# One VectorE operation of 512 columns per sigma in place of two of 256 in a delta-rule attention kernel

## The reference

```
def step(carry, seg):
    mem, z = carry
    qq, kk, vv = seg
    sigma_q = jax.nn.elu(qq) + 1.0
    scores = jnp.einsum('bhsk,bhtk->bhst', qq, kk) / scale
    att_dot = jax.nn.softmax(jnp.where(causal_mask, scores, -jnp.inf), axis=-1) @ vv
    att_mem = sigma_q @ mem / (sigma_q @ z)
    sigma_k = jax.nn.elu(kk) + 1.0
    delta = vv - sigma_k @ mem / (sigma_k @ z)
    mem_new = mem + jnp.einsum('bhsk,bhsv->bhkv', sigma_k, delta)
    z_new = z + sigma_k.sum(axis=-2, keepdims=True).transpose(0, 1, 3, 2)
    att = beta * att_mem + (1.0 - beta) * att_dot
    out = att.reshape(Bsz, SEG, H * DV) @ Wo
```

## Time and profile before

| | |
|---|---|
| median of 3 runs | 744.07 us (743.4 to 746.38) |
| profiled execution, its time | 749.53 us |
| profiled execution, its span | 747.7 us |
| TensorE busy, share of the span | 654.7 us, 88% |
| VectorE busy | 413.3 us, 55% |
| ScalarE busy | 339.4 us, 45% |
| GpSimd busy | 314.3 us, 42% |
| attention | from the start to about 441 us |
| its first stage | about 37 to 90 us |
| its last stage, without sigmas | about 390 to 441 us |

### The profile page before, as it was taken

One profiled execution on the slowest core, in us unless ns is written; L12 is line 12 of the kernel. 1 busy time (PEld: TensorE's weight loads), 2 busy tenths in 40 slices (PEclk: granted clock), 3 DMA queues, 4 the chain that ended last, 5 costly groups with the idle time before them and its releaser, 6 DMA issues. The chain is left out here.

```text
span 747.7 us, 12362 instructions
## 1 busy us (share of the span) xinstructions
PE 654.7 (88%) x4144; PEld 544.1 (73%) x4144; DVE 413.3 (55%) x1119; ACT 339.4 (45%) x834; POOL 314.3 (42%) x383
## 2 busy tenths in 40 slices
PE   4889989989989989989999986999999529984897
PEld 3668878979979879879789885875656318873554
DVE  6778495394593692781873727662222178355233
ACT  3666757566566665665665642123333203000210
POOL 4665644353344435425420305146665318110454
PEclk9999999999999999999999998899999859985799
DMA  8010110200100100100100414942233241028440
GB/s 265 20 57 29 30 56 1 64 29 20 46 29 29 35 28 28 35 28 30 35 1 4 110 64 161 411 145 85 93 85 85 98 153 45 1 77 317 131 113 22
DMA packets 31313, 57.89 MB, mean 77 GB/s; under 512 B 4670, under 2 KB 17952, under 8 KB 31264
## 3 DMA queue, kind: packets, MB, share of 16 engines
q1 hardware_dynamic: 24256, 42.03, 16.7%
q0 software_dynamic: 4896, 13.12, 6.1%
q10 hardware_dynamic: 2112, 2.10, 0.8%
HBM read 48.06 MB, written 10.09 MB: 78 GB/s over the span
## 5 line engine op out<-in xcount | busy, mean ns | idle before, releaser
L892 DVE RECIPROCAL denominators<-readings 128x2 f32<-128x2 f32 x128 | 21.2, 165 | 145.4 <-PE readings L567 144.7
L427 POOL TENSOR_TENSOR w_high<-xn,ones 128x256 fp32r<-128x256 f32 x84 | 53.2, 665 | 76.8 <-PE ahead L215 35.5
L567 PEld LDWEIGHTS readings<-memory_copy,sigma 128*128 128x128 f32 x512 | 75.1, 191 | 13.9 <-ACT memory_copy L764 5.0
L567 PE MATMUL readings<-memory_copy,sigma 128*128 128x129 f32 x512 | 78.9, 276 | 4.0 <-ACT memory_copy L764 3.8
L773 ACT ACTIVATE memory_reading<-readings,denominators 64x128 f32<-64x128 f32 x256 | 78.7, 357 | 5.3 <-DVE denominators L892 3.3
L764 ACT ACTIVATE memory_copy<-memory 128x258 f32<-128x258 f32 x128 | 50.2, 392 | 62.0 <-PE memory L577 48.0
L898 DVE SCALAR_TENSOR_TENSOR minus_delta<-readings,denominators,v 64x128 f32<-64x128 f32 x240 | 73.8, 347 | 4.2
L577 PE MATMUL memory<-minus_delta,sigma_k_tokens 128*128 128x129 f32 x480 | 73.2, 275 | 0.0
L1196 POOL DMA_INDIRECT xs_e<-rows_e,gather_at_e x46 | 44.9, 976 | 65.3 <-DVE scatter_at_e L1597 39.7
L1341 PE MATMUL up_e<-weights_e,xT_e 128*128 x184 | 68.8, 498 | 0.8 <-issue 0.8
L749 ACT ACTIVATE x<-ahead 128x512 f32<-128x512 f32 x60 | 35.9, 598 | 72.9 <-PE ahead L215 28.1
(11 more groups left out here) (267 smaller groups left out, 1438.5 us busy)
## 6 DMA issues: line engine op xcount, KB each, us to landing
weights_e<-experts SPq DMA_DIRECT2D x24, 608.0 KB, 11.8
xn<-L_attn_Wq SPq DMA_DIRECT2D x8, 512.0 KB, 3.8
xn<-L_attn_Wk SPq DMA_DIRECT2D x7, 512.0 KB, 3.8
xn<-L_attn_Wv SPq DMA_DIRECT2D x7, 512.0 KB, 3.9
wo<-L_attn_Wo SPq DMA_DIRECT2D x1, 2048.0 KB, 13.9
rows_e<-xn ACTq DMA_DIRECT2D x4, 512.0 KB, 7.9
x<-L_attn_x SPq DMA_DIRECT2D x4, 256.0 KB, 3.5
x<-L_attn_x SPq DMA_DIRECT2D x2, 512.0 KB, 3.6
```

The costliest lines, as they stand in the source:

```text
L427: last = pool.tensor_tensor(w_high[i][:, :, of], w_stage[:, :, of], one, ALU.mult)
L567: last = pe.matmul(KQ[g][:, hh * MC:(hh + 1) * MC], sqk[:, GROUP * g + hh, pair, 2 * par:2 * par + 2, :], mz[g][:, hh, :], start=True, sto ...
```

## The change

A query's sigma goes into `sigma` in one operation: the destination is blocks 1 and 2 of four tiles, 4 rows of 128 columns. A key's copy is one operation too: its destination is blocks 0 and 3 of four tiles, rows of 64 columns at two distances. The elements, their values and every wait and semaphore are the same; `sigma_ready` is raised by the one operation in place of the second of two.

```
-                def by_segment(t, par):
-                    return t.rearrange("p (a b c) -> p a b c", b=2, c=SEG)[:, :, par, :]
+                def by_segment(t):
+
+                    return t.rearrange("p (t a c) -> p t a c", a=2, c=SEG)
...
-                    for par in range(2):
-                        block_at = 1 + par if i == 0 else 3 * par
-                        out = sqk[:, h, half * TPH:(half + 1) * TPH, block_at, :]
-                        if i:
-                            last = dve.tensor_copy(out, by_segment(sk[h % 2][:, :], par))
-                        else:
-                            last = dve.scalar_tensor_tensor(out=out, in0=by_segment(natural, par), scalar=0.0,
-                                                            in1=by_segment(e[u % 2][:, :], par), op0=ALU.max, op1=ALU.add)
+                    tiles = slice(half * TPH, (half + 1) * TPH)
+                    if i:
+                        last = dve.tensor_copy(sqk[:, h, tiles, 0:4:3, :], by_segment(sk[h % 2][:, :]))
+                    else:
+                        last = dve.scalar_tensor_tensor(out=sqk[:, h, tiles, 1:3, :], in0=by_segment(natural), scalar=0.0,
+                                                        in1=by_segment(e[u % 2][:, :]), op0=ALU.max, op1=ALU.add)
                     last.then_inc(sigma_ready, 1)
```

## The result

| | before | changed |
|---|---|---|
| median | 744.78 us (743.4 to 746.38, 4 runs) | 737.62 us (734.67 to 738.12, 4 runs) |
| ratio, 95% interval | | 0.9891 [0.986, 0.9922] |
| profiled execution's span | 747.7 us | 736.1 us |
| first scores (L588) start at | 37.80 us | 39.80 us |
| first stage, to the next stage's first scores | 48.62 us | 49.43 us |

The medians differ by 7.2 us; by the ratio the change makes the kernel 8.1 us faster (5.8 to 10.4). The stage lengths are read from the timeline: first L588 of a stage to first L588 of the next.

What follows compares the result with a forecast made beforehand. TensorE bounds the kernel, so only its waits on VectorE's queue count. 1.10 us in each of six middle stages (6.6) plus 1.6 in the first stage gives 8.2 off 744.07: 735.9 us, range 732.0 to 740.5.

Steps and rivals of the forecast that it cites:

- What bounds it: Middle stage: TensorE's 2.72 us idle time is three waits of 1.68, 0.40 and 0.64 us, two directly behind sigmas.
- Undisturbed costs: Without GpSimd at work, a merged sigma takes 0.69 us against 0.76 for a pair, a merged copy 0.41 against 0.49.
- estimate of 157 ns: Saving per merged operation by the skill's fixed cost, 2.9 us more in six stages than the rows give; not adopted.
- Disturbed sigmas: Sigmas 2 and 3 beside GpSimd: one wait per operation, 1.10 us each merged, saving 0.38 and 0.60.
- The deduction of 0.18: Taken off each middle stage: L868 comes about 0.5 us earlier and may wait up to 0.42 for a w_low.
- the 1.28 of the sum: Middle stage's saving before deduction: 1.12 us from sigmas 0 to 3, 0.08 each from the copies of sigmas 4 and 5.
- The first stage: Saves 1.6 us: 1.4 from shorter disturbed sigmas 0 and 1, 0.2 of the later 1.39 wait, GpSimd being late next.
- the second rival: Waits for GpSimd only move: middle stages gain nothing, only the first stage keeps some, 743 us; chance 0.08.
- The start: Eight sigmas before the first stage: zero, since TensorE waits for GpSimd's value weights, which each sigma delays as before.
- the room of 3.8 us: Middle stage: GpSimd's probabilities end at 215.63, 3.8 us before TensorE is ready to turn them at 219.42.
- the lost pace: Rival: merged copies take 0.69 us, 0.20 more than the pair, making the kernel 739.7 us; chance 0.08.
- the half pace: Rival: merged sigmas with rows of 128 columns take up to 0.69 us more, making the kernel 754 us; chance 0.03.

## Why the prediction was right, point by point

- **What bounds it**: right. The three waits of a middle stage were where the gain came from: TensorE's idle time there fell from 2.72 to 1.53 us.
- **Undisturbed costs**: 0.69 and 0.43 measured, 0.69 and 0.41 forecast. So a merged operation saves 0.07 and 0.06 us. The trace decides against the estimate of 157 ns that the prediction drew from the Trainium skill, "VectorE: DVE Perf Modes", § The TRN2 errata. That estimate left out what the same page of the Trainium skill adds, § The DRAIN you can't avoid: an operation that is not held starts earlier.
- **Disturbed sigmas**: forecast 1.10 each, measured 0.99 and 1.11. One wait per operation was the right mechanism; the first of them stands beside GpSimd's `w_high` (L427), not `w_low`, and was 0.11 better.
- **The deduction of 0.18** for a lost moment of L868 did not occur: it took 0.41 at its new place as well, by the same luck of the moment as before. In the first stage, where I had not looked, the L869 of sigma 2 lost it and took 1.28 in place of 0.41. So a middle stage gained 1.38, not 1.10, which is the 1.28 of the sum and 0.1 from sigma 2. Six stages: 8.3, forecast 6.6.
- **The first stage** was wrong. Forecast 1.6 gained, 0.8 lost. The step that failed is "I count 1.4" for the two waits on ScalarE: they did vanish, but TensorE then waited 0.67 for GpSimd's `w_low`, and its wait in slot 8 grew from 1.39 to 2.72. TensorE's idle time in the stage is 5.6 us before and after: the waits only moved, as the second rival had it. I had named GpSimd as late next and sized it at nearly nothing. With the full clock the gain is 0.6; the fall of the clock took 1.2 to 1.4 us more.
- **The start** was wrong. Forecast 0 between -0.5 and +0.5, measured 2.0 lost: 1.5 by the clock, and 0.5 by a later value projection (27.60 to 28.10 us), which is no more than what moves there with no edit. The wait ahead of it grew from 1.65 to 2.21 us. The step that failed is that each sigma delays GpSimd "by as much as before": its eight splits there took 6.6 to 6.9 us in the four profiles with pairs at the start, 7.2 to 7.5 in the seven with everything merged, and 5.9 with the queries in quarters. The Trainium skill, "SBUF — State Buffer", § Who interferes with whom, has the loser blocked for the whole of the other's instruction. The rows show the longer holds: a `w_low` beside 512 columns took 1.18 us, and the wait, 2.21 in the changed kernel, was 1.56 with pairs at the start. I had taken from it that the sum of the delays stays the same, and these rows do not bear that out; in the middle stages the room of 3.8 us made it harmless.
- **The clock** had no term at all, and no reason was given for that.
- **The other rivals**: the merged sigma runs at 0.69 and the merged copy at 0.43, so neither the lost pace nor the half pace came true.
- **The whole**: 8.2 forecast, 7.2 measured by the medians and 8.1 by the ratio. By the trace attention gave 5.5. That the total is nearer is luck: by the two profiles it comes from what lies behind attention, which no step of mine accounts for.

## What to carry to other kernels

Before merging operations, look at what the engine beside them does at that moment, here GpSimd: the fixed cost saved here was 0.07 us, the waiting saved up to 0.6. The worth of a shorter operation is that of what stands behind it in its queue, and must be read at each place: the same edit gained 1.4 us per middle stage while 2.8 us were lost in two spots. A gain that makes TensorE early at a late partner can be taken back by the clock behind the longer wait.

## What the runs showed that I had not expected

- A wait of TensorE of 1.8 to 2.8 us inside dense work was often followed by 3.4 us at half clock, at a price of 1.2 to 1.6 us in most stages. The same two places showed it in both profiles of the changed kernel, while waits of 2.84 and 2.32 us in other runs were followed by the full clock.
- In the run with quarters it fell in five middle stages behind two waits of 0.8 to 1.0 us each (0.83 and 0.99 in the stage shown), and not in the sixth, which has the same two.
- What lies behind the last stage's first scores, for the most part the three other layers, took between 333.4 and 340.4 us in fourteen profiles of kernels that do not differ there. It took longer where TensorE spent more of it at half clock (66.3 to 78.6 us).
